# Down projection: GpSimd scales five blocks of the third group and adds the rows of the first two groups; the second group rounded in six pieces

## The chip, the cores and the metric

The kernel runs on one core of a Trainium2 chip. The metric is the device time of one execution in microseconds, lower is better. The core has a matrix engine (TensorE, in the rows PE, and PEld for its weight loads), a vector engine (VectorE, DVE), an activation engine (ScalarE, ACT), a general one (GpSimd, POOL) and a queue that issues DMAs (SyncE, SP, and SPq in the rows). Each engine runs its own instructions in order and waits at semaphores that the others count up.

## What is computed

The reference is one transformer block on x of 8 x 1024 rows of 512 numbers: cross attention to 8 x 64 context rows, then a feed-forward part with fake quantisation. The change concerns the last product of the second part only:

```
def _act_fake_quant(x, clip_factor):
    scale = sigmoid(clip_factor) * max(abs(x)) / 127
    return clip(round(x / scale), -128, 127) * scale
...
xq = _act_fake_quant(layernorm(x), clip_x)
gate, up = xq @ quant(w_gate).T, xq @ quant(w_up).T        # 1408 columns each
h = _act_fake_quant(silu(gate) * up, clip_down)            # one scale for all of h
x = x + h @ quant(w_down).T                                # 1408 -> 512
```

Since h has one scale for the whole tensor, all of h must exist before any of it can be rounded. That splits the feed-forward part into two passes.

## The kernel before

The 8192 rows are taken as NG = 16 groups of 512 rows (GT), a group as TT = 4 tiles of 128 rows. The 1408 hidden columns are FT = 11 blocks of 128. So the hidden values of a group are 11 blocks of 128 partitions x 512, in fp32.

First pass (up to about 1121 us): for each group TensorE makes gate and up sums, ScalarE the silu, VectorE the product and its largest magnitude. Groups 0 to 10 are stored to DRAM (`h_d`); the last five (KEPT = 11 to 15) stay in the five slots of `hb`. Then the scale of h is worked out with one all-reduce by GpSimd over the partitions (`over_partitions(1)`), and VectorE writes `hscale`, which gives the semaphore `down_scales`.

Second pass, the down projection, with a group counter q = 0 to 15 of its own: q = 0 to 4 are the five kept groups, q = 5 to 15 the stored ones, loaded again (`taken_as`). "First", "second", "third group" below are q = 0, 1, 2. For each q:

- ScalarE multiplies each block of the group by its factor and adds a large constant (`MAGIC`), so that the value is rounded (line 1450, in place in `hb`, counted by `h_scaled`). From the third group on it also converts the last two blocks (`BY_SCALAR`, line 1455), once the group before the last is out of the way.
- VectorE (`round_h`) takes away the constant with an upper limit (line 1542, fp32 to bf16 in `hq`, shown as `w`) and clips (line 1546, bf16 to bf16, counted by `h_rounded`). It does so in pieces: block by block (11) for the first group, in three pieces of 4, 4 and 3 blocks for all others (`parts`).
- TensorE (`down_part`, line 1619) multiplies: 11 blocks x 4 row tiles = 44 matmuls per group. Even groups sum in `pu`, odd ones in `pg`, one bank for each row tile. The first two groups go block by block, over the four tiles in each; from the third group on it goes tile by tile, and all 11 blocks of it in each. It waits for `h_rounded` at the first block of each piece.
- VectorE multiplies the sums by the weights' scales, from PSUM to `sg` (`scale_down`, line 1551, counted by `down_taken`).
- The rows x of the group (`x1_d`, loaded to one of four slots, shown as `xa` or `xqT`) are added: tiles 0 and 1 by GpSimd (line 1422, `added`), tiles 2 and 3 by VectorE (`add_rows`, line 1559, `added_too`). Then SyncE stores the slot to the output.

VectorE's order is written out by hand: all pieces of group q + 1 (`round_h`), then the four `scale_down` of q, then `add_rows` of tiles 2 and 3 of q. GpSimd's queue in this pass is nothing but the additions, after the all-reduce.

SyncE's queue is in order, too: load of h for q = 5 (three DMAs, each waits until the same blocks of the group in that slot, q - 5, are rounded), then for each q: load of h for q + 6 (waits for the rounding of q + 1), store of q (waits for its four additions), load of the rows of q + 3 (waits for the landing of the store of q - 1). A group moves 2.75 MB of h, 1 MB of rows and 1 MB of output.

```
for q in range(NG):
    more = q + 1 < NG
    if more:
        for n in range(len(parts(q + 1))):
            round_h(q + 1, n)
    for t in range(TT):
        scale_down(q, t)
        ...
    if more:
        add_rows(q, 2)
        add_rows(q, 3)
```

## Time and profile before

| | us |
|---|---|
| median of 3 runs | 1291.38 (1291.06 to 1292.88) |
| profiled execution, its own time | 1291.84 |
| span of the profiled execution | 1290.0 |
| TensorE busy | 1254.6 (97%) |
| VectorE busy | 1110.9 (86%) |
| ScalarE busy | 802.1 (62%) |
| GpSimd busy | 288.0 (22%) |

The down projection is the stretch from 1124.4 to the end. Times in rows are microseconds from the start of the span, durations of single instructions in nanoseconds where a row says so. An instruction that waits for something shared with another engine is shown with a longer duration, while one that waits at a semaphore starts later: its idle time stands in square brackets with what ended it. "x4" merges instructions of one line, the duration is then that of the whole row from the first start to the last end. A busy TensorE is a model of pipelined matmuls. The granted clock of TensorE is 1.00 of full speed all through the down projection.

### The profile page before, as it was taken

What the parts mean: (1) busy time and instruction counts of PE and PEld (TensorE: products, weight loads), DVE (VectorE), ACT (ScalarE), POOL (GpSimd) and SP (SyncE); (2) the same over time, 40 slices, a digit from 0 to 9 for tenths busy, and PEclk for the clock granted to TensorE, in tenths of its full rate; (3) what the DMA queues carried; (4) which work ended last, traced back from release to release, by engine and by line L of the source; (5) the groups of instructions that cost most, each with busy time, mean ns of one, the idle gap of its engine ahead of it and who ended that gap; (6) DMA issues with size and microseconds to landing.
All of it is one profiled execution on the core that took longest, in us unless ns stands there. A gap on an engine that the chain in (4) does not pass through costs nothing.

```text
span 1290.0 us, 20436 instructions
## 1 busy us (share of the span) xinstructions
PE 1254.6 (97%) x7563; PEld 586.0 (45%) x7607; DVE 1110.9 (86%) x2117; ACT 802.1 (62%) x1211; POOL 288.0 (22%) x227
## 2 busy tenths in 40 slices
PE   6999799999999999999999999999999999989998
PEld 4644344444444444444444444444444444434443
DVE  7776979887988988898889868899999999889998
ACT  6588576587567757755875671334334334499993
POOL 2103421441343144224413420000000000012223
PEclk9999899999999999999999999999999999999999
DMA  8285146356246265462563391387656742399997
GB/s 302 77 242 172 34 115 212 87 149 208 73 131 205 72 187 135 115 212 67 163 215 97 98 272 60 87 280 265 228 205 260 251 141 70 111 340 418 420 418 303
DMA packets 182436, 241.74 MB, mean 187 GB/s; under 512 B 122032, under 2 KB 141248, under 8 KB 169920
## 3 DMA queue, kind: packets, MB, share of 16 engines
q1 hardware_dynamic: 182336, 240.43, 56.2%
q8 instruction: 60, 0.98, 0.3%
q14 instruction: 40, 0.33, 0.1%
HBM read 120.86 MB, written 90.57 MB: 164 GB/s over the span
## 4 chain that ended last, share of the span: by engine, by line
PE 78%; ACT 8%; DMA 7%; DVE 5%; issue 2%; SPq 1%; POOL 0%; DVEq 0%
PE pg L1586 11%; PE pu L1592 11%; PE po L77 9%; PE po L79 9%; PE po L78 9%; PE ring L79 7%; PE ring L77 7%; PE ring L78 7%; ACT hb L1450 4%; PE ring L1055 2%; PE ring L1082 2%; DMA out_dram<-xqT 2%; DMA out_dram<-xa 1%; DMA x<-in_x_dram 1%; DMA xqT<-x_rows_d 1%
## 5 line engine op out<-in xcount | busy, mean ns | idle before, releaser
L1428 ACT ACTIVATE sg<-pg,gate_scale 128x512 f32<-128x512 f32 x176 | 120.9, 687 | 183.5 <-PE pg L1586 183.5
L77 PE MATMUL ring<-yT,M 128*128 128x512 f16 x512 | 194.1, 379 | 0.0
L78 PE MATMUL ring<-yT,M 128*128 128x512 f16 x512 | 194.0, 379 | 0.0
L79 PE MATMUL ring<-yT,M 128*128 128x512 f16 x512 | 194.0, 379 | 0.0
L77 PE MATMUL po<-VW,p 128*128 128x512 f16 x480 | 182.9, 381 | 1.5 <-DVE p L667 1.5
L78 PE MATMUL po<-VW,p 128*128 128x512 f16 x480 | 182.4, 380 | 0.0
L79 PE MATMUL po<-VW,p 128*128 128x512 f16 x480 | 182.4, 380 | 0.0
L1586 PE MATMUL pg<-xqT,w 128*128 128x512 bf16 x690 | 178.8, 379 | 1.8 <-ACT xqT L1439 0.8
L1592 PE MATMUL pu<-xqT,w 128*128 128x512 bf16 x689 | 178.6, 379 | 0.8
L469 ACT ACTIVATE p<-E 128x512 f16<-128x512 f32 x120 | 75.0, 625 | 129.3 <-DVE E L663 129.3
L1502 DVE TENSOR_TENSOR hb<-pu,sg 128x512 f32<-128x512 f32 x176 | 120.9, 687 | 26.5 <-PE pu L1592 25.0
L394 POOL TENSOR_TENSOR esum<-esum,E 128x512 f32<-128x512 f32 x96 | 130.3, 1357 | 30.1 <-ACT E L458 17.9
L1450 ACT ACTIVATE hb<-hb,magic,hscale 128x512 f32<-128x512 f32 x176 | 125.6, 802 | 3.9 <-DVE hscale L1531 3.9
L391 POOL TENSOR_TENSOR esum<-E 128x512 f32<-128x512 f32 x16 | 23.6, 1475 | 444.7 <-DVE p L667 399.4
L1506 DVE TENSOR_REDUCE hmax_g<-hb 128x1 f32<-128x512 f32 x176 | 117.8, 677 | 0.0
L1586 PEld LDWEIGHTS pg<-xqT,w 128*128 128x128 bf16 x704 | 68.7, 98 | 84.4 <-DMA xqT<-xq 1.3
L1592 PEld LDWEIGHTS pu<-xqT,w 128*128 128x128 bf16 x704 | 68.9, 98 | 83.1
L667 DVE TENSOR_TENSOR p<-E,p 128x512 f16<-128x512 f32 x120 | 82.5, 688 | 19.3 <-ACT p L469 19.1
L448 ACT ACTIVATE E<-ring,score_bias,score_scale 128x512 f32<-128x512 f32 x128 | 97.6, 762 | 0.0
L458 ACT ACTIVATE E<-E,score_bounds 128x512 f32<-128x512 f32 x128 | 91.8, 717 | 2.5
L454 ACT ACTIVATE E<-E,score_bounds 128x512 f32<-128x512 f32 x128 | 91.4, 714 | 1.2
L663 DVE SCALAR_TENSOR_TENSOR E<-E,pd 128x512 f32<-128x512 f32 x128 | 85.9, 673 | 0.5
(238 smaller groups left out, 1991.0 us busy)
## 6 DMA issues: line engine op xcount, KB each, us to landing
hidden<-hb SPq DMA_DIRECT2D x11, 2816.0 KB, 9.1
xa<-x_rows_d SPq DMA_DIRECT2D x28, 1024.0 KB, 5.7
hb<-hidden SPq DMA_DIRECT2D x22, 1024.0 KB, 16.1
x<-in_x_dram SPq DMA_DIRECT2D x16, 1024.0 KB, 6.2
value_fold<-E SPq DMA_DIRECT2D x64, 256.0 KB, 2.5
VW<-value_fold SPq DMA_DIRECT2D x16, 1024.0 KB, 5.9
x_rows_d<-x SPq DMA_DIRECT2D x16, 1024.0 KB, 4.1
out_dram<-xa SPq DMA_DIRECT2D x11, 1024.0 KB, 12.8
```

The lines of the kernel that those rows point to most:

```text
L77: nc.tensor.matmul(out, a_hi, b_hi, start=first, stop=False)
L78: nc.tensor.matmul(out, a_hi, b_lo, start=False, stop=False)
L79: return nc.tensor.matmul(out, a_lo, b_hi, start=False, stop=last)
L394: nc.gpsimd.tensor_tensor(esum[:], esum[:], E[:, g % 2, t], ALU.add).then_inc(sums, 1)
L448: nc.scalar.activation(E[:, g % 2, t], ring[t % 4][:], ACT.Relu, scale=keep.score_scale[:], bias=keep.score_bias[:, k:k + 1]).then_inc(cap ...
L458: nc.scalar.activation(E[:, g % 2, t], E[:, g % 2, t], ACT.Exp, bias=keep.bounds[:, 1:2]).then_inc(exps, 1)
L1428: nc.scalar.activation(sg[:, n % 4], pg[n % 4][:], ACT.Silu, scale=gate_scale[:, n % FT:n % FT + 1]).then_inc(silus, 1)
L1450: nc.scalar.activation(hb[:, slot, m], hb[:, slot, m], ACT.Identity, scale=hscale[:, m:m + 1], bias=magic[:, 0:1]).then_inc(h_scaled, 1)
L1502: nc.vector.tensor_tensor(hb[:, HOME[g], i], pu[n % 4][:], sg[:, n % 4], ALU.mult).then_inc(hs, 1)
L1506: nc.vector.tensor_reduce(hmax_g[:, i:i + 1], hb[:, HOME[g], i], AX.X, ALU.max, apply_absolute_value=True).then_inc(reaches, 1)
L1586: ins = nc.tensor.matmul(pg[n % 4][:], wg[:, c, at], xqT[:, g % 2, c], start=(c == 0), stop=(c == DC - 1))
L1592: ins = nc.tensor.matmul(pu[n % 4][:], wu[:, c, at], xqT[:, g % 2, c], start=(c == 0), stop=(c == DC - 1))
```

## The change

Three things change, all in the down projection:

- GpSimd, after the all-reduce and after `down_scales`, scales blocks 6 to 10 of the third group (q = 2) in place, the operation that ScalarE did, and counts `h_scaled_too`. ScalarE scales only blocks 0 to 5 of this group. Who uses blocks 6 to 10 waits for the new semaphore as well.
- For q = 0 and 1 GpSimd adds the rows of all four tiles; VectorE's `add_rows` begins at q = 2. The counts of `added` and `added_too` are written anew (`added_at`, `by_pool`).
- The second group (q = 1) is rounded in six pieces of 1, 1, 2, 2, 2 and 3 blocks in place of three. Behind each of the last four pieces VectorE does one `scale_down` of the first group, in place of all four after the last piece. The loads of h keep their three parts (`THIRDS`, `rounded_to`).

```diff
@@ -1285,6 +1285,7 @@
     r_loaded = [sem(f"r_loaded{k}") for k in range(4)]
     out_stored = [sem(f"out_stored{k}") for k in range(4)]
     down_scales, h_scaled, h_step, h_rounded = sem("down_scales"), sem("h_scaled"), sem("h_step"), sem("h_rounded")
+    h_scaled_too = sem("h_scaled_by_pool")
     downs, down_taken, added, added_too = sem("downs"), sem("down_taken"), sem("added_by_pool"), sem("added_by_dve")
     og = out.rearrange("b (j t p) d -> (b j) p t d", j=2, p=P)
     FIRST_ORDER = (2, 0, 1, 3)
@@ -1294,8 +1295,14 @@
     taken_as = lambda q: KEPT + q if q < 5 else q - 5
     h_slot = lambda q: HOME[KEPT + q % 5]
     BY_SCALAR = (FT - 2, FT)
-    scaled_by = lambda q, m: (FT * q + m if q < 2 else 2 * FT + (FT + 2) * (q - 2) + m)
-    parts = lambda q: tuple((m, m + 1) for m in range(FT)) if q == 0 else ((0, 4), (4, 8), (8, FT))
+    BY_POOL = 6
+    THIRDS = ((0, 4), (4, 8), (8, FT))
+    scaled_by = lambda q, m: (FT * q + m if q < 2 else 2 * FT + min(m, BY_POOL) + max(m - FT, 0) if q == 2 else
+                              2 * FT + BY_POOL + 2 + (FT + 2) * (q - 3) + m)
+    parts = lambda q: (tuple((m, m + 1) for m in range(FT)), ((0, 1), (1, 2), (2, 4), (4, 6), (6, 8), (8, FT)), THIRDS)[min(q, 2)]
+    rounded_to = lambda q, m: parts_before(q) + [m1 for m0, m1 in parts(q)].index(m) + 1
+    by_pool = lambda q, t: q < 2 or t < 2
+    added_at = lambda q, t: 4 * q + t + 1 if q < 2 else (2 * q + 4 + t + 1 if t < 2 else 2 * (q - 2) + t - 1)
     parts_before = lambda q: sum(len(parts(k)) for k in range(q))
     sums_of = lambda q: pu if q % 2 == 0 else pg
     def wait(eng, s, v):
@@ -1355,8 +1362,8 @@
                 sp.dma_start_transpose(xqT[:, g % 2, :, t * P:(t + 1) * P], xq[:, t]).then_inc(x_turned[g % 2], 16)
 
         def load_h(q):
-            for n, (m0, m1) in enumerate(parts(1)):
-                sp.wait_ge(h_rounded, m1 if q == 5 else parts_before(q - 5) + n + 1)
+            for m0, m1 in THIRDS:
+                sp.wait_ge(h_rounded, rounded_to(q - 5, m1))
                 sp.dma_start(hb[:, h_slot(q), m0:m1], h_d[taken_as(q)][:, m0:m1]).then_inc(h_loaded[h_slot(q)], 16)
 
         def load_r(q):
@@ -1389,15 +1396,13 @@
                 load_h(q + 6)
             slot = (2 + q) % 4
             if q < NG - 1:
-                sp.wait_ge(added, 2 * q + 2)
-                sp.wait_ge(added_too, 2 * q + 2)
+                sp.wait_ge(added, added_at(q, 3 if q < 2 else 1))
+                if q >= 2:
+                    sp.wait_ge(added_too, added_at(q, 3))
                 sp.dma_start(og[taken_as(q)], xa[slot]).then_inc(out_stored[slot], 16)
             else:
                 for t in range(TT):
-                    if t < 2:
-                        sp.wait_ge(added, 2 * q + t + 1)
-                    else:
-                        sp.wait_ge(added_too, 2 * q + t - 1)
+                    sp.wait_ge(added if by_pool(q, t) else added_too, added_at(q, t))
                     sp.dma_start(og[taken_as(q)][:, t], xa[slot][:, t]).then_inc(out_stored[slot], 16)
             if 0 < q < NG - 3:
                 load_r(q + 3)
@@ -1414,10 +1419,13 @@
 
         over_partitions(0)
         over_partitions(1)
+        pool.wait_ge(down_scales, 1)
+        for m in range(BY_POOL, FT):
+            nc.gpsimd.tensor_scalar(hb[:, h_slot(2), m], hb[:, h_slot(2), m], hscale[:, m:m + 1], MAGIC, ALU.mult, ALU.add).then_inc(h_scaled_too, 1)
         for q in range(NG):
             slot = (2 + q) % 4
             pool.wait_ge(r_loaded[slot], 16 * (q // 4) + 16)
-            for t in range(2):
+            for t in range(4 if q < 2 else 2):
                 pool.wait_ge(down_taken, 4 * q + t + 1)
                 nc.gpsimd.tensor_tensor(xa[slot][:, t], xa[slot][:, t], sg[:, t], ALU.add).then_inc(added, 1)
 
@@ -1445,11 +1453,13 @@
         for q in range(NG):
             slot = h_slot(q)
             if q >= 5:
-                act.wait_ge(h_loaded[slot], 16 * len(parts(1)) * (q // 5))
-            for m in range(FT):
+                act.wait_ge(h_loaded[slot], 16 * len(THIRDS) * (q // 5))
+            for m in range(BY_POOL if q == 2 else FT):
                 nc.scalar.activation(hb[:, slot, m], hb[:, slot, m], ACT.Identity, scale=hscale[:, m:m + 1], bias=magic[:, 0:1]).then_inc(h_scaled, 1)
             if q > 1:
                 act.wait_ge(h_scaled, scaled_by(q, FT))
+                if q == 2:
+                    act.wait_ge(h_scaled_too, FT - BY_POOL)
                 wait(act, downs, 4 * (q - 1))
                 for m in range(*BY_SCALAR):
                     nc.scalar.activation(hq[:, q % 2, m], hb[:, slot, m], ACT.Identity, bias=magic[:, 1:2]).then_inc(h_scaled, 1)
@@ -1538,6 +1548,8 @@
             by_scalar = q > 1 and m1 == FT
             last = BY_SCALAR[0] if by_scalar else m1
             dve.wait_ge(h_scaled, scaled_by(q, last))
+            if q == 2 and last > BY_POOL:
+                dve.wait_ge(h_scaled_too, last - BY_POOL)
             wait(dve, downs, 4 * (q - 1))
             nc.vector.tensor_scalar(hq[:, q % 2, m0:last], hb[:, h_slot(q), m0:last], MAGIC, QMAX, ALU.subtract, ALU.min).then_inc(h_step, 1)
             dve.wait_ge(h_step, parts_before(q) + n + 1)
@@ -1547,7 +1559,8 @@
 
         def scale_down(q, t):
             dve.wait_ge(downs, 4 * q + t + 1)
-            wait(dve, added if t < 2 else added_too, 2 * (q - 1) + t % 2 + 1)
+            if q > 0:
+                dve.wait_ge(added if by_pool(q - 1, t) else added_too, added_at(q - 1, t))
             nc.vector.tensor_tensor(sg[:, t], sums_of(q)[t][:], down[:], ALU.mult).then_inc(down_taken, 1)
 
         def add_rows(q, t):
@@ -1565,11 +1578,13 @@
             if more:
                 for n in range(len(parts(q + 1))):
                     round_h(q + 1, n)
-            for t in range(TT):
+                    if q == 0 and n >= 2:
+                        scale_down(q, n - 2)
+            for t in range(TT if q > 0 else 0):
                 scale_down(q, t)
                 if t >= 2 and not more:
                     add_rows(q, t)
-            if more:
+            if more and q >= 2:
                 add_rows(q, 2)
                 add_rows(q, 3)
```

## Rows read from the trace of the kernel before

**Rows 1.** Windows of all engines; columns: busy us and instructions, PEclk, DMA share, GB/s.
```profile
1125.00:1155.00 30.00, 26.04 (x118) 11.12 (x118) 26.02 (x47) 29.97 (x44) 5.04 (x4) 1.00 0.79 282
1155.00:1271.00 116.00, 112.15 (x510) 50.33 (x520) 110.51 (x144) 112.53 (x161) 32.55 (x24) 1.00 1.02 417
```

**Rows 2.** The chain that ended last, in order of time: start, us, what.
```profile
1246.05 14.41 DMA xqT<-x_rows_d
```

**Rows 3.** Timeline of TensorE, group 14: start, us, engine, line, operation, idle before.
```profile
1265.95 1.02 PE L1619 MATMUL pu<-w 128*128 128x512 bf16 x4 [1.36 <-DVE w L1546]
...
1267.95 8.65 PE L1619 MATMUL pu<-w 128*128 128x512 bf16 x39 [0.98 <-DVE w L1546]
```

**Rows 4.** Windows of 1 us at the start of the down projection.
```profile
1129.00:1130.00 1.00, 1.00 (x7) 0.47 (x5) 0.93 (x4) 1.00 (x2) 0.00 (x0) 1.00 0.83 139
...
1137.00:1138.00 1.00, 0.82 (x4) 0.40 (x5) 0.13 (x2) 1.00 (x3) 0.00 (x0) 1.00 0.13 49
...
1146.00:1147.00 1.00, 0.85 (x4) 0.20 (x2) 1.00 (x2) 1.00 (x2) 0.00 (x0) 1.00 0.36 148
```

**Rows 5.** Timeline of the first three groups of the down projection.
```profile
1124.44 23.40 ACT L1450 ACTIVATE hb<-hb,magic,hscale 128x512 f32<-128x512 f32 x33 [3.87 <-DVE hscale L1531]
1125.35 0.43 DVE L1542 TENSOR_SCALAR w<-hb 128x512 bf16<-128x512 f32 x1 [0.30 <-ACT hb L1450]
1125.82 0.29 DVE L1546 TENSOR_SCALAR w<-w 128x512 bf16<-128x512 bf16 x1
1126.03 0.42 DVE L1542 TENSOR_SCALAR w<-hb 128x512 bf16<-128x512 f32 x1
...
1126.26 9.66 PE L1619 MATMUL pu<-w 128*128 128x512 bf16 x43 [0.59 <-DVE w L1546]
...
1128.24 13.77 SPq L1360 DMA_DIRECT2D hb<-hidden  x6
...
1137.18 9.67 PE L1619 MATMUL pg<-w 128*128 128x512 bf16 x43 [1.26 <-DVE w L1546]
...
1139.25 0.69 DVE L1546 TENSOR_SCALAR w<-w 128x2048 bf16<-128x2048 bf16 x1
...
1141.58 2.48 DVE L1551 TENSOR_TENSOR sg<-pu,down 128x512 f32<-128x512 f32 x4
1142.42 2.52 POOL L1422 TENSOR_TENSOR xqT<-xqT,sg 128x512 f32<-128x512 f32 x2 [18.67 <-DVE sg L1551]
...
1146.16 0.39 SPq L1394 DMA_DIRECT2D out_dram<-xqT  x1
...
1148.10 1.02 PE L1619 MATMUL pu<-w 128*128 128x512 bf16 x4 [1.25 <-DVE w L1546]
...
1149.87 8.87 PE L1619 MATMUL pu<-w 128*128 128x512 bf16 x39 [0.75 <-DVE w L1546]
```

**Rows 6.** Timeline of VectorE and GpSimd at one place of the down projection.
```profile
1248.48 0.69 DVE L1559 TENSOR_TENSOR xa<-xa,sg 128x512 f32<-128x512 f32 x1 [1.34 <-DMA xa<-x_rows_d]
...
1248.53 1.78 POOL L1422 TENSOR_TENSOR xa<-xa,sg 128x512 f32<-128x512 f32 x1 [8.39 <-DMA xa<-x_rows_d]
...
1249.09 1.76 DVE L1559 TENSOR_TENSOR xa<-xa,sg 128x512 f32<-128x512 f32 x1
...
1250.27 1.72 POOL L1422 TENSOR_TENSOR xa<-xa,sg 128x512 f32<-128x512 f32 x1
...
1250.78 2.29 DVE L1542 TENSOR_SCALAR w<-hb 128x2048 bf16<-128x2048 f32 x1
```

**Rows 7.** Durations of single lines (ns: min/median/max), and one row of GpSimd's timeline.
```profile
L1422 POOL TENSOR_TENSOR xa<-xa,sg x24: 1263/1277/1778, 1151.5 to 1284.0; 128x512 f32<-128x512 f32 x24
...
L1542 DVE TENSOR_SCALAR w<-hb x56: 419/1214/2299, 1125.4 to 1276.6; 128x2048 bf16<-128x2048 f32 x30, 128x512 bf16<-128x512 f32 x25, 128x1536 bf16<-128x1536 f32 x1
...
L399 POOL COPY yT<-cT x8: 1092/1116/2119, 24.1 to 32.4; 128x512 f16<-128x512 f16 x8
...
L701 DVE TENSOR_SCALAR row_scale<-row_scale x11: 169/1215/1286, 151.4 to 598.2; 128x2 f32<-128x2 f32 x11
...
773.36 0.38 POOL L1409 PARTITION_ALL_REDUCE one<-magic  x1 [5.79 <-issue]
```

## The prediction

> **What bounds the kernel now.** I read the table of windows first, because the change touches only the last 165 us (the down projection, from 1124.4). From 1155 to 1271 the DMA share is 1.02 at 417 GB/s, in the thirty microseconds before it is 0.79 at 282 GB/s [rows 1]. So the reader is to see two stages: a first one in which the DMA engines still have holes, and a second, 116 us long, in which they have none. TensorE is nearly full in both, so it is no guide by itself. The chain of work that ended last says which one counts: it passes from DMA to DMA, the last time through the load of group 12's rows, 14.41 us from issue at 1246.05 to landing at 1260.46 [rows 2]. Only after that landing can VectorE add its rows and round group 14, and TensorE then waits 1.36 and 0.98 us for it [rows 3]. From that landing to the end of the span there are 29.5 us of work with nothing else in them. So the end moves with the landing, and the landing moves with the holes in the DMA stream ahead of 1155, one for one, since behind them the stream is full and carries a fixed number of bytes. A delay or gain of TensorE counts in full only as far as it outlasts the 2.3 us of waiting in [rows 3].
>
> The holes, in windows of 1 us: the stream starts in 1129 to 1130 (share 0.83), although the first load, part one of group 5's hidden block, is issued at 1128.24 [rows 4, 5]: about 0.95 us from issue to flow, estimated from these two. It stands still in 1137 to 1138 (share 0.13) and in 1146 to 1147 (0.36) [rows 4], because the next request came late: group 6's first part waits for the second group's first four blocks to be rounded, and group 0's output store (1146.16) waits for its last addition [rows 5]. With the latency these two holes are 1.0 us each, 2.0 us together. TensorE's own waits at this place are 1.26 before the second group, 1.25 before the third and 0.75 inside it, 3.26 us [rows 5].
>
> **The change, part by part.**
>
> What it takes away. Six pieces in place of three let TensorE begin the second group once one block of it is rounded: its 1.26 goes. ScalarE scales 28 blocks in place of 33 up to the third group: 23.40/33 = 0.709 us each [rows 5], so 3.5 us earlier. VectorE loses four additions, 0.69 us each where nothing holds them [rows 6]. If nothing else happened, TensorE would gain its 3.26 us, and the DMA stream its 2.0.
>
> What it puts in. GpSimd gets five scalings of 128x512, at the very moment at which VectorE starts the first group's rounding, and four additions each for the first two groups in place of two. The rows at 1248 show what an operation of GpSimd costs VectorE [rows 6]. VectorE's first addition runs in 0.69. GpSimd's beside it takes 1.78 in place of the usual 1.277 [rows 7]. VectorE's second takes 1.76, GpSimd's second 1.72, and the rounding behind it (line 1542, four blocks) 2.29 in place of a median of 1.21 [rows 7]. Each of them ends as if it had begun 0.14 us before the end of the one ahead: the two engines take turns, one whole instruction each. A multiplication out of PSUM (line 1551) isn't held: four in 2.48 us with GpSimd adding [rows 5]. Even the TENSOR_SCALAR of two numbers at line 701 has a median of 1215 ns and a minimum of 169 [rows 7]. So every TENSOR_SCALAR of VectorE pays the whole rest of a GpSimd operation.
>
> The price of one scaling by GpSimd has no row. The nearest is its copy of 128x512 with one input, median 1.116 us; the addition with two inputs is 1.277 [rows 7]. I take 1.12; the ends are 1.28 and 0.56, half of the copy. The page GPSIMD Engine Reference of the Trainium skill (3.1, Elementwise) has a tight one-input loop over 512 elements at 0.77 us. By that the sum below, as an estimate, would be 3.8 and not 5.3 us. No run shows which it is.
>
> First group. GpSimd begins at 1124.5 and has five operations; VectorE gets in one of its two operations per block between each. Each is held 1.12 - 0.14 = 0.98 us by the one ahead. The turns: scaling 1 to 1125.6, rounding to 1125.9, scaling 2 to 1126.9, limiting to 1127.1, and so on; the fifth scaling ends at 1130.5. Then two and a half blocks at 0.68 us each (line 1542 starts at 1125.35 and again at 1126.03 [rows 5]) bring block 3 to 1131.7, where it was 1128.24 (the issue of the load that waits for it). **3.5 us later** starts the load of group 5, the head of the DMA stream. The first group is rounded at 1136.5 in place of 1133.1 (1125.35 + 11 x 0.709), and TensorE, which needs 0.87 us per block (9.66 us for 11 [rows 5]), ends it at 1139.1 in place of 1135.9.
>
> Second group. ScalarE is far ahead by now; VectorE is not. Two pieces of one block at 0.69 and one of two blocks (line 1542 0.69 and line 1546 0.43, estimated between the 0.43/0.29 of one block and the 1.22/0.69 of four [rows 5, 7]) end at 1139.0. From there each piece comes with a multiplication out of PSUM, which releases an addition by GpSimd. VectorE's line 1542 is first, the addition next, and line 1546 behind it. The period is 0.62 + 0.62 + 1.14 + 0.29 = 2.67 us: pieces end at 1141.7, 1144.35 and, with three blocks (0.62 + 0.89 + 1.14 + 0.42), 1147.4. Blocks 4 to 7 are rounded at 1144.35; before it was 1139.94 (1139.25 + 0.69 [rows 5]). The fourth addition falls behind the third group's first rounding and ends at 1147.4 + 0.62 + 1.16 + 1.14 = 1150.3; group 0's store was at 1146.16. Here the new order of VectorE costs more than its two lost additions gave.
>
> Third group. Its rounding ends its parts at 1150.9 (1150.3 - 0.14 + 0.69), 1152.8 and 1153.7; before, TensorE could begin on it at 1148.10 [rows 5]. TensorE now: second group from 1139.1, held 1.4 us before block 8, over at 1150.2; third from 1150.95, held 0.95 and 0.15, over at 1161.7 (9.66 and the two holds), in place of 1158.65 (1149.87 [rows 5] and 40/44 of 9.66). That is 3.1 us later and not 3.26 earlier. The third scaling itself costs ScalarE nothing; GpSimd's are done at 1130.5. GpSimd's additions to group 1 hold the fourth group's first two roundings and end at 1161.0. Nothing in them stops TensorE for more than some tenths.
>
> DMA stream. A group's three parts, alone, flow for 8.0 us (1129.2 to 1137.1). It starts 3.5 later. The old hole before group 6's first part goes (issued 1139.0, stream busy to 1140.6), and that before the store as it was, together -2.0. New ones: group 6's second part is issued at 1144.4 and flows from 1145.35, with the stream empty from 1143.6: 1.75, and 0.15 before its third; group 0's store, issued 1150.35, 0.7; group 1's store, issued 1161.0 behind 9.4 us of queued work from 1151.3, 1.2. **Sum: 3.5 - 2.0 + 1.9 + 0.7 + 1.2 = 5.3 us later.** That is more than TensorE's delay, and decides. Each turn in the first group moves all that follows, so five times the change of a scaling is the change of the sum: 6.1 with scalings of 1.28, 2.5 to 2.8 with 0.56.
>
> Bookkeeping. The span of the profiled execution is 1290.0, its time 1291.84; the median of three is 1291.38. I add 5.3 to the median: 1296.7. The span goes to 1295.3.
>
> **The rivals.**
>
> *A, the turns don't happen at the short operations.* No row shows line 1546 (bf16 to bf16) beside a busy GpSimd. If it isn't held, the second group's last pieces are over at 1141.5 and 1143.6, the store goes at 1146.5, and the stream is 1.4 us later: 1292.8. For it: no row. Against it: the same kind of instruction, and the two numbers of line 701. The Trainium skill (SBUF, State Buffer: Who interferes with whom) counts a tensor_scalar in the fast bf16 mode among those that block fully, which speaks against the change, too. Chance 0.12.
>
> *B, the other side.* GpSimd's operations lie in gaps of VectorE or hold it for a fraction. Then the two holes close and TensorE's 3.26 us go. The stream gives 1.3 to 2.0: 1289.4 to 1290.1. It would be faster by more than 2.6 us only if the landing did not bind, too: then 3.3, 1288.1. The point at which it turns: a hold of under about 0.2 us per turn in place of 1.0. Against it are the long rows of lines 1542 and 1559 [rows 6]. Chance 0.12, of that 0.05 below 1288.8.
>
> *C, GpSimd starts late.* At 767 its first all-reduce stood still for 5.79 us with nothing to wait for that the profile shows [rows 7], as if it had to make something ready. If the way back to plain operations costs the same, the scalings run from 1129.6 to about 1136.5, over blocks 6 to 10. Group 5's first part is in time, the second 3.5 us late; the rest of the reckoning, done as above, gives 6.1 to 6.8: 1297.5 to 1298.2. Until now it would have lain in GpSimd's idleness before its first addition. Chance 0.14.
>
> *D, the DMA stream has play.* It moved 282 GB/s in the first stage and could make up some of the delay by fuller windows; then TensorE decides, 3.1 later less the 2.3 it waits at group 14: 0.8, 1292.2. Chance 0.12.
>
> **How the numbers follow.** Forecast as reckoned (scaling 0.56 to 1.28, 1294.0 to 1297.5): 0.50, time 1296.7. A measurement of this kernel can tell 0.2%, 2.6 us, from no change. Slower by more: forecast, and C: 0.62, with some of the low end lost. Same: A, D, most of B: 0.33. Faster: 0.05. The range leaves out B's faster half and what is over 1298.4: 1290.0 to 1298.4.
>
> **What would show it.** In the new profile: five GpSimd operations at 1124.5 of 1.1 to 1.3 us; lines 1542 and 1546 with means well over 0.43 and 0.29 in the first blocks; the first load of hidden blocks issued near 1131.7; the second group's last piece near 1147; the third group's matmuls over near 1161.7; the row load of group 12 landing near 1265.8. If GpSimd's operations last 0.6, or lines 1542/1546 keep their old lengths, the forecast is wrong at the first step. If these hold and the end still moves by under 2 us, it is wrong at the stream.

## The result

Measured in turn on one chip, fifteen executions each, the changed kernel takes 1294.76 us (1293.64 to 1296.89) and the kernel before 1292.08 us (1290.81 to 1293.84). The ratio is 1.0021, 95% interval 1.0013 to 1.0028: 2.7 us slower, a small difference of about 0.2%, but one whose interval leaves out "no change". The direction was as forecast and the time is within the range. The forecast of 5.3 us was twice what came.

The profiled execution of the changed kernel is the slowest of its fifteen (1296.89, span 1295.1). Its down projection also starts 0.49 us later than before's, for reasons ahead of the change, so places are compared below by their distance from the first matmul of the down projection: 1126.26 before [rows 5], 1126.75 now.

**What the prediction's rows have become.** First the timeline of the first groups, changed kernel (start, us, engine, line, operation, in brackets the idle time before it and what ended it). Line 1554 is the old 1542, 1558 the old 1546, 1424 the new scaling, 1430 GpSimd's addition, 1634 the matmuls.

```profile
1123.88 0.35 POOL L1418 PARTITION_ALL_REDUCE one<-one  x1 [312.73 <-DVE one L1537]
...
1124.66 0.23 DVE L1541 TENSOR_SCALAR hscale<-hscale,one 128x11 f32<-128x11 f32 x1
...
1126.75 9.66 PE L1634 MATMUL pu<-w 128*128 128x512 bf16 x44 [0.60 <-DVE w L1558]
...
1131.82 4.50 POOL L1424 TENSOR_SCALAR hb<-hb,hscale 128x512 f32<-128x512 f32 x5 [7.58 <-issue]
1131.89 0.76 DVE L1558 TENSOR_SCALAR w<-w 128x512 bf16<-128x512 bf16 x1
1132.57 0.41 DVE L1554 TENSOR_SCALAR w<-hb 128x512 bf16<-128x512 f32 x1
1133.01 0.59 DVE L1558 TENSOR_SCALAR w<-w 128x512 bf16<-128x512 bf16 x1
...
1137.09 0.43 DVE L1558 TENSOR_SCALAR w<-w 128x1024 bf16<-128x1024 bf16 x1
...
1138.04 0.68 DVE L1554 TENSOR_SCALAR w<-hb 128x1024 bf16<-128x1024 f32 x1
1138.56 1.29 POOL L1430 TENSOR_TENSOR xqT<-xqT,sg 128x512 f32<-128x512 f32 x1 [2.24 <-DVE sg L1564]
1138.76 1.38 DVE L1558 TENSOR_SCALAR w<-w 128x1024 bf16<-128x1024 bf16 x1
...
1140.20 1.90 PE L1634 MATMUL pg<-w 128*128 128x512 bf16 x8 [0.33 <-DVE w L1558]
...
1142.81 1.90 PE L1634 MATMUL pg<-w 128*128 128x512 bf16 x8 [0.71 <-DVE w L1558]
...
1145.82 2.76 PE L1634 MATMUL pg<-w 128*128 128x512 bf16 x12 [1.11 <-DVE w L1558]
...
1148.65 0.39 SPq L1402 DMA_DIRECT2D out_dram<-xqT  x1
...
1151.09 8.87 PE L1634 MATMUL pu<-w 128*128 128x512 bf16 x40 [0.75 <-DVE w L1558]
...
1152.71 6.42 POOL L1430 TENSOR_TENSOR xa<-xa,sg 128x512 f32<-128x512 f32 x4 [4.09 <-DVE sg L1564]
...
1157.91 2.29 DVE L1554 TENSOR_SCALAR w<-hb 128x2048 bf16<-128x2048 f32 x1
...
1159.15 0.39 SPq L1402 DMA_DIRECT2D out_dram<-xa  x1
```

Three readings. GpSimd stands still for 7.58 us behind its all-reduce and only then scales: five in 4.50 us. The first 0.66 us of it pass until VectorE has written the scale, for which the scaling waits; for the other 6.9 us the profile shows nothing that it waits for. VectorE's clipping beside it takes 0.59 (0.29 before [rows 5]) and, with an addition of GpSimd ahead of it, 1.38 where the two blocks alone take 0.43. TensorE's wait before the second group (1.26 [rows 5]) is gone as an entry, but 0.33, 0.71 and 1.11 inside it have come, 2.15 us together. And two outputs are stored later: group 0's at 21.9 us behind the first matmul (19.9 before [rows 5]), group 1's at 32.4. In the kernel before that was 29.0:

```profile
1155.23 0.39 SPq L1394 DMA_DIRECT2D out_dram<-xa  x1
```

The chain that ended last (start, us, what) still goes through DMAs, and the load of group 12's rows still ends the waiting: issued 122.7 us behind the first matmul, before 119.8 [rows 2]. Changed kernel:

```profile
1249.41 15.12 DMA xqT<-x_rows_d
```

And TensorE's timeline of group 14, which waits for it:

```profile
1270.01 1.38 PE L1634 MATMUL pu<-w 128*128 128x512 bf16 x4 [2.06 <-DVE w L1558]
...
1271.79 9.86 PE L1634 MATMUL pu<-w 128*128 128x512 bf16 x40 [0.39 <-DVE w L1558]
```

The waits there are 2.06 and 0.39 ([rows 3]: 1.36 and 0.98), and the 40 matmuls take 9.86 us where 8.87 is usual (1151.09 above).

**The DMA stream, aligned.** Windows of 20, 13, 17 and 70 us from the first matmul on; the last two columns are DMA share and GB/s. The kernel before:

```profile
1126.26:1146.26 20.00, 18.63 (x85) 8.31 (x88) 16.46 (x33) 20.00 (x29) 2.52 (x2) 1.00 0.78 285
1146.26:1159.26 13.00, 10.95 (x50) 4.56 (x50) 12.80 (x18) 12.94 (x20) 2.52 (x2) 1.00 0.95 346
1159.26:1176.26 17.00, 16.95 (x79) 7.71 (x79) 16.86 (x22) 16.93 (x25) 5.01 (x4) 1.00 1.03 421
1176.26:1246.26 70.00, 69.63 (x319) 31.76 (x325) 67.80 (x91) 69.77 (x101) 18.95 (x14) 1.00 1.02 419
```

The changed kernel:

```profile
1126.75:1146.75 20.00, 17.85 (x81) 7.64 (x82) 19.45 (x37) 19.97 (x29) 9.67 (x9) 1.00 0.71 249
1146.75:1159.75 13.00, 11.51 (x53) 4.80 (x52) 12.86 (x13) 12.97 (x20) 8.29 (x5) 1.00 0.98 351
1159.75:1176.75 17.00, 16.84 (x78) 7.38 (x77) 16.80 (x24) 16.93 (x25) 5.01 (x4) 1.00 0.99 377
1176.75:1246.75 70.00, 69.95 (x325) 31.52 (x322) 67.42 (x87) 69.07 (x100) 19.46 (x14) 1.00 1.02 419
```

Rate times width: in the first 50 us 5.70 + 4.50 + 7.16 = 17.36 MB before and 4.98 + 4.56 + 6.41 = 15.95 MB now. The 1.41 MB between them are 3.4 us at 419 GB/s, and in the 70 us behind, both flow at 419. So in this kernel the lag arises in the first 50 us and is carried on as it is: group 12's rows are first added 137.8 us behind the first matmul, where it was 134.2. Half of it (0.72 MB) is there after 20 us, ahead of the late stores, the other half comes in the third window (0.75 MB), behind group 1's late store.

### The profile page after: what moved, and what is told of

It is laid out like the page before. It is cut to its first block, busy times and chain, and to the rows that moved or that the text cites. A ratio compares the mean times of both kernels' runs of the same rounds, so it can differ in the third digit from the quotient of the medians.

```text
span 1295.1 us, 20482 instructions
## 1 busy us (share of the span) xinstructions
PE 1260.8 (97%) x7607; PEld 587.0 (45%) x7607; DVE 1115.8 (86%) x2119; ACT 798.1 (62%) x1206; POOL 301.4 (23%) x236
## 4 chain that ended last, share of the span: by engine, by line
PE 75%; ACT 8%; DVE 7%; DMA 5%; issue 2%; SPq 1%; POOL 0%; DVEq 0%
PE pg L1601 10%; PE pu L1607 10%; PE po L77 9%; PE po L79 9%; PE po L78 9%; PE ring L77 7%; PE ring L79 7%; PE ring L78 7%; ACT hb L1458 4%; PE ring L1055 2%; PE ring L1082 2%; DMA out_dram<-xa 1%; DMA out_dram<-xqT 1%; DMA xqT<-x_rows_d 1%; SPq L1362 1%
## 5 line engine op out<-in xcount | busy, mean ns | idle before, releaser
L391 POOL TENSOR_TENSOR esum<-E 128x512 f32<-128x512 f32 x16 | 23.6, 1477 | 444.4 <-DVE p L667 399.0
L1458 ACT ACTIVATE hb<-hb,magic,hscale 128x512 f32<-128x512 f32 x171 | 122.0, 802 | 5.9 <-DVE hscale L1541 3.9
```

Of the source, the lines that this page charges most:

```text
L1458: nc.scalar.activation(hb[:, slot, m], hb[:, slot, m], ACT.Identity, scale=hscale[:, m:m + 1], bias=magic[:, 0:1]).then_inc(h_scaled, 1)
```

## The experiments

The runs are told here by kind. On record first were e1 to e4, then e5 to e8, then e9 and e10, and last e11 and e12. Four theories stood. (1) GpSimd's additions, taking turns with VectorE, delay the stores and the loads of h, and the end moves with the DMA stream. (2) The scaling by GpSimd costs it all. (3) Only TensorE's path decides; the stream has play. (4) The interleaved order of the six pieces is what costs. Theory 4 came only with e5 to e8, and for these theory 1 was restated by what e1 to e4 had shown: the head of the stream has play, and the lag counts from where the stream fills up. So its hits in e5 to e8 are those of the restated theory. Ratios are to the kernel before in the same runs, with 95% intervals.

### One part undone

**e1, additions as before** (the rest of the change stays):

```
-    by_pool = lambda q, t: q < 2 or t < 2
+    by_pool = lambda q, t: t < 2
...
-            if more and q >= 2:
+            if more:
                 add_rows(q, 2)
```

> The changed kernel with one part undone: VectorE adds tiles 2 and 3 of the first two groups again, GpSimd only tiles 0 and 1, as before. Scaling by GpSimd and the six pieces stay. Theory 1 (the turns that GpSimd's additions take between VectorE's roundings delay group 0's store and the loads of h, and the end moves with the holes in the DMA stream): by the same reckoning as in the prediction, now with the scaling that the changed kernel's trace shows (0.68 us, from 7.6 us behind the all-reduce), store of group 0 near 1147 and of group 1 near 1156 (us from the start of the span), stream 1.9 us later than before: ratio to before about 1.0015, against 1.0021 to 1.0026 for the whole change. Theory 2 (the scaling by GpSimd and its late start cost it all): still 2.7 us, 1.0021. Theory 3 (only TensorE's path decides): third group over 0.8 us later, less than its waits at group 14: 0.

Measured: 1.0016 (1.0007 to 1.0025), 2.1 us. Group 1's store is at 1154.54, 29.2 us behind the first matmul (1125.35): its delay is gone. Yet most of the time stays. The aligned windows give 0.9 us of lag (246, 380 and 420 GB/s: 17.00 MB). In the profile 1.6 us more come in group 14, where the matmuls are stretched (39 in 10.27 us, 8.65 before [rows 3]):

```profile
1268.45 10.27 PE L1633 MATMUL pu<-w 128*128 128x512 bf16 x39 [0.98 <-DVE w L1557]
```

**e2, scaling as before** (`BY_POOL = FT`, no instruction of GpSimd and no wait for it):

> The changed kernel with ScalarE scaling all eleven blocks of the third group again; GpSimd adds all rows of the first two groups, six pieces. Theory 1: VectorE is free in the first group, but the additions keep taking turns with it in the second: the second group's last piece near 1144.8, group 0's store near 1147.7, stream 2.7 us later, of 4.0 by the same reckoning for the whole change; measured perhaps two thirds of each, ratio about 1.0014 to 1.002. Theory 2: nothing is left, ratio 1.000 or below. Theory 3: below 1 us, since the third group's matmuls are over 0.2 us later only.

Measured: 1.0016 (1.0007 to 1.0024), 2.6 us by the medians. Group 1's store is 32.0 us behind the first matmul (1158.08 less 1126.11). Theory 2 falls: without any scaling by GpSimd 2.6 of the 2.7 us are still there (by the ratios 1.0016 of 1.0021).

**e3, three pieces as before:**

```
-    parts = lambda q: (..., ((0, 1), (1, 2), (2, 4), (4, 6), (6, 8), (8, FT)), THIRDS)[min(q, 2)]
+    parts = lambda q: (..., THIRDS, THIRDS)[min(q, 2)]
```

> The changed kernel with the second group rounded in three pieces again and the first group's four multiplications out of PSUM behind them. Theory 1: the rounding of the second group is no longer held (its parts near 1137.1, 1140.0 and 1141.7, as before), but four additions by GpSimd in a row stand at 1.25 us each beside the third group's rounding: group 0's store near 1148.9, group 1's near 1158.9, stream 3.4 us later by the reckoning, ratio 1.0015 to 1.0026. Theory 2: as the whole change, 1.0021. Theory 3: third group over 0.8 us later, 0.

Measured: 1.0026 (1.0018 to 1.0035), 3.3 us, the slowest of the three, store of group 1 at 32.8. Taking the six pieces back saves nothing while GpSimd still adds all rows; theory 3, with 0, missed here. It is not the end of it, though: in this profile TensorE's clock is at half for twice as long as elsewhere, in the third group (39 matmuls in 11.65 us), which its reckoning didn't have. e9 and e10 put it to the test.

### One part alone

**e5, the additions alone:**

> The kernel before with one part of the change: GpSimd adds all four tiles of the first two groups, VectorE none of them. No scaling by GpSimd, three pieces. Theory 1, as the first four runs leave it (the head of the stream has play; the lag counts from where the stream fills up, about 27 to 50 us behind the first matmul of the pass, and then stays to the end): four additions in a row by GpSimd put group 0's store near 22.7 us behind the first matmul (before 19.9) and group 1's near 32.7 (before 29.0); lag 3.4 to 4.1 us, ratio 1.0025 to 1.003. Theory 2 (scaling costs it): 0.

Measured: 1.0027 (1.0017 to 1.0037), 3.8 us by the medians. One part makes at least as much as the whole (1.0021, 1.0013 to 1.0028; the intervals overlap). The timeline of this kernel (GpSimd and the stores), and behind it its aligned windows:

```profile
1142.76 6.40 POOL L1427 TENSOR_TENSOR xqT<-xqT,sg 128x512 f32<-128x512 f32 x4 [18.68 <-DVE sg L1559]
...
1149.18 0.39 SPq L1402 DMA_DIRECT2D out_dram<-xqT  x1
...
1159.35 0.39 SPq L1402 DMA_DIRECT2D out_dram<-xa  x1
```

```profile
1126.60:1146.60 20.00, 18.73 (x87) 8.31 (x88) 16.43 (x32) 20.00 (x29) 3.84 (x3) 1.00 0.80 286
1146.60:1159.60 13.00, 10.19 (x39) 4.00 (x38) 12.90 (x12) 12.94 (x20) 8.95 (x6) 0.87 0.75 269
1159.60:1176.60 17.00, 17.00 (x80) 7.73 (x79) 16.83 (x23) 16.94 (x25) 5.00 (x4) 1.00 1.01 383
```

Four additions stretch over 6.40 us. The same four tiles of rows shared between two engines took from 1142.42 to 1146.08 before. Group 0's store is 2.7 us later counted from the first matmul, group 1's 3.8, and in the 13 us around them the stream runs at a share of 0.75 and 269 GB/s. 15.73 MB in 50 us: 3.9 us of lag. (The 0.87 in the second row is TensorE's granted clock; see the part on the clock.)

**e7, the scaling alone:**

> The kernel before with the scaling of the third group's blocks 6 to 10 by GpSimd alone. GpSimd idle for about 7.6 us behind its all-reduce, then five operations at 0.9 us beside VectorE's last blocks of the first group; VectorE's later wait for ScalarE before the second group takes the delay up. Theory 1: lag 0 to 0.3 us, ratio 1.000 (0.999 to 1.0005). Theory 2: 2.7 us, 1.002.

Measured: 1.0002 (0.9993 to 1.0011). The five operations are there, behind the same standstill, and cost nothing:

```profile
1131.30 4.11 POOL L1423 TENSOR_SCALAR hb<-hb,hscale 128x512 f32<-128x512 f32 x5 [7.18 <-issue]
```

VectorE still waits 0.68 and 0.87 us for ScalarE before its next pieces (shown as its idle time at line 1553 of this kernel), so the delay of the first group's rounding had a cover.

**e6, the pieces alone:**

> The kernel before with the six pieces alone (and the four multiplications of the first group between them); additions shared as before, ScalarE scales everything. Theory 1: two of GpSimd's additions fall between pieces and hold them; store of group 0 near 19.4 behind the first matmul, lag 0 to 0.6 us, ratio 1.000 to 1.0005. Theory 4 (the interleaved order is what costs): at least half of the change's 2.7 us, ratio over 1.001.

Measured: 1.0010 (1.0001 to 1.0019), 1.5 us by the medians, more than theory 1 said and at the lower edge of what theory 4 asked. The stores are early (group 1's 28.3 behind the first matmul). Two additions of GpSimd fall between pieces and hold them, the second part of group 6's h is issued later, and the windows give 0.7 us of lag (260, 371 and 414 GB/s: 17.06 MB). The profile has a stretched group 14 here as well:

```profile
1267.86 10.49 PE L1628 MATMUL pu<-w 128*128 128x512 bf16 x40 [0.75 <-DVE w L1552]
```

**e8, the pieces alone, and GpSimd's two additions of group 0 held until the fourth multiplication is done:**

```
-                pool.wait_ge(down_taken, 4 * q + t + 1)
+                pool.wait_ge(down_taken, 4 * q + (4 if q == 0 else t + 1))
```

> As the six pieces alone, but GpSimd's two additions of the first group wait for the fourth multiplication, so that none stands between pieces. Theory 1: pieces near 1136.3, 1139.8, 1141.9 (before's time), TensorE's 1.26 us before the second group gone; group 0's store near the old place, since the additions come later and hold the third group's first rounding: lag -0.3 to 0, ratio 0.9995 to 1.000. A version that would be better than both could only be a little better.

Measured: 0.9992 (0.9983 to 1.0001). Against e6 only the place of two additions differs, and 1.8 us of the medians go with it. So the pieces by themselves cost nothing, and theory 4 falls. By what path the two additions cost, the traces answer otherwise than theory 1: group 12's rows are first added 135.8 us behind the first matmul in e6 and 135.6 in e8, hardly a difference, and the last group begins at 153.4 and 151.6. What lies between is group 14, which e8 runs at the usual pace:

```profile
1268.74 8.87 PE L1628 MATMUL pu<-w 128*128 128x512 bf16 x40 [0.75 <-DVE w L1552]
```

So in these two profiles 1.6 us of the difference are the fall of the clock. Whether that holds for the executions behind the medians no run shows. e8 is the fastest version that computes everything, 0.3 us under the median of the kernel before, which the interval does not separate from it.

### The stream itself

**e4, the kernel before with group 5's load of h held back** until the whole first group is rounded:

```
-                sp.wait_ge(h_rounded, m1 if q == 5 else parts_before(q - 5) + n + 1)
+                sp.wait_ge(h_rounded, FT if q == 5 else parts_before(q - 5) + n + 1)
```

> The kernel before with one edit: the three loads of group 5's h wait until all 11 blocks of the first group are rounded (1133.1) in place of 4, 8 and 11. No engine's work changes, only the DMA stream starts 4.9 us later. Theory 1 (the stream's holes count one for one): it swallows the two old holes of 1.0 us each, so 2.9 us later, ratio 1.0022, and the row load of group 12 lands near 1263.4 in place of 1260.5. Theory 3 (the stream has play, TensorE decides): 0, ratio 1.000.

Measured: 1.0001 (0.9993 to 1.0010). Theory 1 missed. The aligned windows say why:

```profile
1126.92:1146.92 20.00, 18.64 (x85) 8.34 (x88) 16.46 (x33) 20.00 (x29) 2.51 (x2) 1.00 0.61 243
1146.92:1159.92 13.00, 10.95 (x42) 4.33 (x42) 12.79 (x18) 12.93 (x20) 2.50 (x2) 0.87 1.02 396
1159.92:1176.92 17.00, 16.95 (x80) 7.74 (x79) 16.86 (x22) 16.93 (x25) 5.02 (x4) 1.00 1.03 420
```

It is 0.84 MB behind after 20 us, and 0.21 MB (0.5 us) after 50. The second window flows at 396 where the kernel before had 346. The clock at 0.87 is not the reason: the unchanged kernel with the same fall (e11) has 351 there. The held-back requests were waiting and the stream moved more in the same time, so this hole at the head was mostly made up while the next requests came in time. Both stores stand where they stood (29.0 for group 1). Behind a store in SyncE's in-order queue stand the next rows and the next h, so a late store holds back these as well. That this is why late stores cost is argued, not shown: no run holds back a store and nothing else.

**e9 and e10, both kernels with lighter row loads.** Of the rows of groups 4 to 11 only the first of four tiles is loaded, so the other rows added there are not the right ones:

```
+            t1 = 1 if 4 <= q < 12 else TT
-            sp.dma_start(xa[slot], x1_d[taken_as(q)]).then_inc(r_loaded[slot], 16)
+            sp.dma_start(xa[slot][:, 0:t1], x1_d[taken_as(q)][:, 0:t1]).then_inc(r_loaded[slot], 16)
```

> The kernel before with the row loads of groups 4 to 11 of the down projection cut to the first tile of four (three quarters of 8 MB left out, some 15 us of the stream at 420 GB/s); the rows of the other tiles are stale. All engines do the same work. Theory 1 (the DMA stream binds the end): the row load of group 12 lands in time, TensorE's waits at groups 13 and 14 (3.3 us) go, 1288 to 1289, ratio 0.9975. If the stream doesn't bind: 1.000.

> The changed kernel with the same row loads cut. Theory 1: the stream no longer binds either, so only TensorE's path is left: its third group is over about 1 us later than before, counted from the first matmul of the pass. Against the uncut kernel before: ratio 0.998 to 0.9985, 0.8 to 1.2 us above the cut kernel before and not 2.7. Theory 3 (the engines' path costs the 2.7 us, whatever the stream does): 2.7 us above the cut kernel before.

Measured: 0.9965 (0.9951 to 0.9978), 1288.56 us, for the kernel before, and 0.9976 (0.9966 to 0.9986), 1289.16 us, for the changed one. So the stream binds the end in both: they gain 3.5 and 5.6 us by the medians. With it out of the way TensorE has no wait at all from the third group on (e9, last groups):

```profile
1254.62 9.66 PE L1620 MATMUL pg<-w 128*128 128x512 bf16 x44
1264.12 9.66 PE L1620 MATMUL pu<-w 128*128 128x512 bf16 x44
1273.62 9.66 PE L1620 MATMUL pg<-w 128*128 128x512 bf16 x44
```

The two kernels are then 0.6 us apart by the medians and 1.4 by the ratios, in place of 2.7. The two intervals overlap, with five and eight executions, so this remainder is not a sure one. Theory 3, which asked for 2.7, falls on it. The remainder is TensorE's own path, and the clock stands against it: e9's profile has half the clock in its third group (40 matmuls in 10.41 us), e10's, at 8.88, has not. In these profiles the last group begins 147.8 us behind the first matmul in e9 and 147.5 in e10; without e9's 1.5 us of lost clock the changed kernel would be 1.2 us the later one (an estimate from these rows). The rest of the 2.7 came through the waits for the stream, the fall of the clock in group 14 included, which e10, without these waits, no longer has.

### The clock

**e11 and e12, both kernels again, unchanged, one profiled execution each:**

> The kernel before, unchanged, for a second profiled execution. The first had the granted clock of TensorE at 1.00 all through the down projection; four of the kernels with long waits at group 14 (the changed one, and those with the adds undone, the scaling undone, the pieces alone) had it at half speed for 3.4 us in that group, which stretched its matmuls from 9.5 to 11.1 us or so. Theory 5 (the longer or differently placed waits of the changed kernel bring that fall, a second cost beside the stream's lag): none here, group 1's store again 29.0 us behind the first matmul of the pass, landing of group 12's rows 134.2 behind it. If the fall comes here too, it belongs to the execution and not to the kernel.

> The changed kernel, unchanged, for a second profiled execution. Theory 1: the stream's lag repeats: group 1's store 32.4 us behind the first matmul (3.4 more than before), the load of group 12's rows issued 122.7 behind it (before 119.8), GpSimd idle 7 to 7.6 us behind the all-reduce and then five scalings. Theory 5: the half-speed stretch comes at group 14 again; if it doesn't, the end is 1.2 to 1.6 us earlier counted from the first matmul.

Measured: spans 1290.0 and 1294.5; group 1's store at 29.0 and 32.5 us behind the first matmul. The granted clock (third from the end) of the changed kernel falls again in group 14 (q = 14) and that of the kernel before doesn't; first e11, then e12:

```profile
1265.00:1275.00 10.00, 8.39 (x38) 3.58 (x39) 9.88 (x14) 2.22 (x4) 2.50 (x2) 1.00 1.02 398
```
```profile
1265.00:1275.00 10.00, 7.75 (x29) 2.84 (x28) 9.90 (x12) 3.33 (x5) 4.65 (x4) 0.83 1.03 408
```

0.83 over ten microseconds is 3.4 us at the lower of the two levels, 1.2 in place of 2.4 GHz. Matmuls that take half the clock for 3.4 us lose up to 1.7 us. Ahead of the fall TensorE had waited 1.18 and 0.75 us in group 13 and 2.03 in group 14.

But the kernel before is not free of the fall. In e11 it comes in the third group, where the first profile had 8.87 us for this row:

```profile
1149.19 10.49 PE L1619 MATMUL pu<-w 128*128 128x512 bf16 x40 [0.75 <-DVE w L1546]
```

So theory 5 held for group 14 and missed the rest: the fall is no property of the changed kernel, but the place where it comes differs. All profiles with the full stream, us; "store" is group 1's and "lag" the missing bytes of the first 50 us at 419 GB/s, both against the first profile of the kernel before; "rows" is when group 12's rows are first added, behind the first matmul, and "then" the time from there to the first matmul of the last group:

| kernel | pieces | store | lag | rows | then | clock at half in |
|---|---|---|---|---|---|---|
| before | 3 | 0 | 0 | 134.2 | 15.96 | nowhere |
| before again (e11) | 3 | 0.0 | -0.1 | 134.8 | 15.94 | third group |
| late load (e4) | 3 | 0.0 | 0.5 | 135.1 | 15.94 | third group |
| scaling alone (e7) | 3 | 0.3 | 0.3 | 134.8 | 15.94 | nowhere |
| additions alone (e5) | 3 | 3.8 | 3.9 | 137.9 | 15.94 | third group |
| pieces undone (e3) | 3 | 3.8 | 4.1 | 138.6 | 15.94 | third group |
| changed | 6 | 3.4 | 3.4 | 137.8 | 16.92 | group 14 |
| changed again (e12) | 6 | 3.5 | 3.5 | 137.9 | 16.83 | group 14 |
| scaling undone (e2) | 6 | 3.0 | 2.8 | 137.0 | 17.57 | group 14 |
| additions undone (e1) | 6 | 0.2 | 0.9 | 135.6 | 17.57 | group 14 |
| pieces alone (e6) | 6 | -0.7 | 0.7 | 135.8 | 17.57 | group 14 |
| pieces alone, additions behind (e8) | 6 | -0.4 | -0.3 | 135.6 | 15.95 | nowhere |

Four things can be read from it. The end hangs on the landing of group 12's rows: from there to the last group it is 15.94 to 15.96 us wherever the clock stays up in group 14, whatever the change. Where it falls there, 0.9 to 1.6 us are added, and nothing behind makes them up. A fall in the third group is taken back from TensorE's later waits for the stream: in group 13 it waits 0.27 us in e11 and 0.98 in the first profile, and both spans are 1290.0. And in these profiles the fall came in the third group only with three pieces and in group 14 only with six; why it skips from the one to the other no run shows, and how long TensorE waited in group 14 doesn't decide it, since e6 and e8 wait alike (1.19 and 0.75 us, 1.21 and 0.75).

The table leaves one thing open. In e1, e6 and e8 the rows come 0.8 to 1.6 us later than in the two profiles of the kernel before, though their lag after 50 us is 0.9 at most. Something behind these 50 us costs them time, and the bytes don't show what.

How often the clock falls in executions without a profile is open, too: three of the fifteen times of the changed kernel lie at 1296.65 and above, the other twelve at 1295.66 and below, which would suit a fall in some of them, but nothing here shows it.

## Why the prediction was right, and where its sizes were off

- **What bounds the kernel.** Right: with 6 MB less in the stream the end comes 3.5 us earlier (e9), and a lag once made stays at 419 GB/s (aligned windows). The time from the landing of group 12's rows to the last group is the same within 0.02 us in seven profiles. "One for one" holds behind the first 50 us only.
- **Turns of whole instructions.** Right for the additions, the bf16 clipping included: 1.38 us in place of 0.43 between additions. Rival A falls, and rival B as far as the additions go. The Trainium skill (SBUF, State Buffer: Who interferes with whom) counts such a clipping among the instructions that block fully, and the trace agrees (1.38 for 0.43).
- **One operation of VectorE between two scalings.** Wrong. Between two scalings VectorE got both its operations of a block in: the clipping was held (0.59 for 0.29), the rounding ran in its usual 0.41. Its blocks came 0.95 us apart beside the scalings (starts of line 1554 at 1132.57, 1133.52, 1134.48) and 0.71 without, so a scaling cost VectorE 0.24 us and not 0.98, which is near the 0.2 of rival B.
- **The price of a scaling.** Off: 0.68 us for the first, alone, and not 1.12; with VectorE in between they come 0.95 us apart. The copy was the wrong neighbour. The Trainium skill's figure for a one-input loop (GPSIMD Engine Reference, 3.1, Elementwise) was 0.77 and nearer. (By the prediction's own rule, five times the change of a scaling, its sum with 0.77 would have been 3.55 and not 3.8.)
- **When the scaling starts.** This was rival C, with a chance of 0.14: 7.58 us of standstill where it had reckoned 5.79, so the five operations met the last blocks of the first group. With the true duration they cost nothing (e7), and not 6.1 us.
- **The 3.5 us at the head of the stream.** The step that failed, twice over: group 5's first load was issued on time (2.0 us behind the first matmul in both kernels, 1128.24 before [rows 5], 1128.73 now), and had it come late, e4 shows that 4.9 us there cost 0.1 us by the ratio. It was the term that carried two thirds of the forecast. (The reckoning is loose here, too: two and a half blocks of 0.68 behind 1130.5 end at 1132.2 and not at 1131.7.) Rival D was right on this point, though not in its conclusion (0.8 us).
- **The second group's pieces.** The period of 2.67 us per piece came out as 2.61 to 2.62 (starts of line 1564 at 1137.44, 1140.06, 1142.67). But the delay of TensorE was far too large: the third group was to be over 3.1 us later and was 0.7 us later (its 40 matmuls began 24.3 us behind the first one, before 23.6), since the first group was not held up.
- **The stores.** Right in kind and too small in weight. "Group 1's store, 1.2" was one of the smaller terms, while the table shows it as the mark that the lag follows: late by 3.0 to 3.8 us with a lag of 2.8 to 4.1 in five profiles, and by at most 0.3 with a lag of at most 0.9 in the others. That the late store is itself the cause, and not a companion of it, was not isolated.
- **The sum.** That it came within a factor of two is luck. A head of 3.5 us that counts for nothing stood against a lag from stores and pieces that was forecast at 1.8 us (the sum without the head) and measured at 3.4.
- **What was not in the sum.** The fall of the clock in group 14, 0.9 to 1.6 us in a profile that has it. The forecast took the clock as constant. In the profiled span of 1295.1, which the forecast of 1295.3 seems to hit, it stands in for terms that weren't there; the median shows the true gap.

## What to carry to other kernels

Before work is moved to GpSimd for an engine that has too much, count what its instruction does to VectorE's fast ones beside it, and ask which queue waits for the last of the moved pieces. Here two tiles of four, moved off VectorE, made a store late, and the DMA stream behind it did not make that up (e5: 3.8 us later, 3.9 us of lag). A hole in a stream is not worth its length: 4.9 us at the head cost next to nothing (e4), while a lag that was there when the stream was full stayed. A part that is free alone and a part that costs can hide in one change, and their costs don't add up: additions alone 3.8 us, pieces alone 1.5, scaling alone nothing that can be measured, all three 2.7. And look at the granted clock of all stages in both profiles, and in a second profile of each: the same fall is free where the engine has play and costs up to 1.6 us where it has none.

## What the runs showed of the hardware

- From a partition all-reduce back to a plain operation GpSimd stood still for 6.94 to 7.90 us in six profiles (e3 the least, e1 the most). The first 0.66 us of each are the wait for the scale; for 6.3 to 7.2 us the profile shows nothing that it waited for. Before the change nothing was queued there, and it could not be seen.
- GpSimd's multiply-add of 128x512 fp32 with one input took 0.68 us undisturbed; its addition of two takes 1.277 [rows 7].
- Beside these multiply-adds VectorE got two short operations in between each two, and in the changed kernel only the clipping was held (0.59 us for 0.29). In four other profiles (e1, e7, e10, e12) the first rounding beside them was held as well, 0.89 to 0.97 us for 0.43.
- The DMA engines moved 346 GB/s at a share of 0.95 in the 13 us around the first stores and 419 at 1.02 in the full stage, and 396 at 1.02 in those 13 us when the first load had come late (e4).
- TensorE's granted clock fell to half for 3.4 us in group 14 in five of twelve profiles with the full stream, and in the third group in four others (for about 6.8 us in e3). In e12 it fell behind waits of 1.18 and 0.75 us in the group ahead and 2.03 there. Three profiles had no such fall.
